# Three PSUM banks for each kind of score in the feature attention, and a new instruction order in the grouped-query attention of a decoder kernel

## The chip, the cores and the metric

The kernel runs on one core of one Trainium2 chip. The time is the device time of one execution in microseconds; the number reported is the median of the runs. A difference of less than 0.2% (about 6 us here) can't be told from no change.

## The reference

Two pre-norm layers over x of 64 x 64 x 256 values, each x = x + block(layernorm(x)). The change touches the first two of the six blocks.

```python
# block 1: grouped-query attention, 16 query heads, 4 key heads of 128, causal
q, k, v = split(x @ w_qkv.T)
q = layernorm(q) * g + b; k = layernorm(k) * g + b      # per head
q = q * cos + rotate_half(q) * sin                      # k the same
attn = softmax(causal(q @ k.T / sqrt(128))) @ v
x = x + attn @ w_o.T
# block 2: attention over features, 8 heads of 8 positions
qh, kh, vh = (a.reshape(b * 8, 64 // 8, 256) for a in (q, ctx, ctx))
sm = softmax(einsum('bdm,bdn->bmn', qh, kh) / sqrt(8))  # 256 x 256 scores
x = x + einsum('bmn,bcn->bcm', sm, vh).reshape(b, 64, 256)
```

## The kernel before

The 64 sequences are 32 tiles of 128 rows (two sequences). x stays in SBUF (`x_all`). Each block runs over the 32 tiles with one instruction stream per engine, written by hand, and counted semaphores between them. `over_tiles` (L35) unrolls two tiles (block 1) or four (block 2) per loop turn; in the source `t` is the tile and `step(t, ...)` the code of a tile on one engine. What stands in `step` on each engine is the order of the work; a wait is `wait_ge(semaphore, count)`, and `wait_used` (L48) is the wait for a buffer to be free.

**Block 1, `attention_gqa` (L545).** In step t, the scores and softmax of tile t run beside the projections of tile t+1 (the names `keys`, `value`, `queries`, `square_keys`, `keys_raw`, `rotate_query` with t+1), the output projection of tile t-1 (`at_.values`, `at_.project`) and the transposed layernorm rows of tile t+2. PSUM's eight banks are all in use; `QBANK` gives the banks 2, 1, 0, 3 to the four groups g of four query heads. On TensorE (PE) the step opens with `keys` (L103 to L105 with a_wk), `value`, the eight transposes of the probabilities of t-1 (L391), `query_sums` (L904, L905: sums of squares that give each query's variance), `bias_scores` (L896: the part of the scores that comes from the layernorm's bias, needed only at `s2m`), `key_sums` (L867), `scores` (L916), and then values, queries and projections. VectorE (DVE) runs `keys_raw` (L744, L745), the variance `vq` (L796), `keys_summed` (L750, L752), `s2m` (L800), the statistics of t+2, the scaled scores s (L809, L814), `low` (L437, the low half of an fp16 split), `take_max` (L357), then the query rotation: `rotate_query` (L764) and `add_swapped` (L769) for four groups, the denominator (L375), and `ln.low` (L280), which releases the next tile's `keys`. GpSimd (POOL) raises vq to the power -1/2 (L645, `rq`), does the same for the keys, then `swapped_part` (L627) and `squares_low` (L632) per group, `subtract_max` (L361) and `normalise` (L381). ScalarE (ACT) reads each query group out of PSUM: two squares (L684, L685) and two copies that swap halves (L688, qsw); between groups 1 and 2 stand the exponential (L370), the copy of v (L678) and the second `high` (L431, the high half of the split), and at the end `ln.high` (L276).

**Block 2, `attention_features` (L1159).** A tile has XU = 16 units (one head of one sequence). Softmax needs a maximum per column before the exponential, so each unit's scores are computed twice: raw scores of tile t+1 (L1458, then the maximum on DVE, L1394) and, with the maxima fed back through DRAM as a row of q, shifted scores of tile t (L1462, then the exponential on ACT, L1363), which PE issues in alternation in `both_scores`. At step u of tile t PE does the raw scores of the unit u+4 of tile t+1 and the shifted scores of the unit u+2 of tile t. `wait_scores` waits until the maximum has left the raw bank, `wait_shifted` until the exponential has left the shifted bank. Every second step adds `values` (L1495, the weighted sums, 0.62 us for eight matmuls), and the steps 11 and 13 one half each of `gather_output` (L1519). Banks 0 to 3 hold raw scores, 4 and 5 shifted ones, 6 the sums and 7 the gathered output and the negated maxima. ACT interleaves with its 16 exponentials: `shifts` (L1340, the negated maxima), `values_out` (L1346, twice, each behind a `values` of PE), and after the exponential of unit 14 `inverse_out` (L1351), which waits for PE's second gather, issued in step 13. The ring `e` of ES = 8 buffers lets the exponential of a unit u that is a multiple of four start only behind the `values` of the group two before it.

```python
s1_ps = lambda u: ps[:, u % 4, :].rearrange("p (c n) -> p c n", n=DM)
s2_ps = lambda u: ps[:, 4 + u % 2, :]
...
if not (isinstance(t, int) and XU * t + u < 4):
    pe.wait_ge(mx_ready, XU * t + u - 3)
...
if not (isinstance(t, int) and XU * t + u < 2):
    pe.wait_ge(e_ready, XU * t + u - 1)
```

## Time and profile before

| what | value |
|---|---|
| median of 3 runs | 3075.42 us (3070.69 to 3077.81) |
| the profiled execution | 3078.19 us, its span 3076.4 us |
| block 1, from its first to its last scores | about 72 to 892 us, 32 tiles, 26.4 us from tile to tile |
| block 2 | about 940 to 1406 us, 32 tiles, 13.37 us from tile to tile in most of it |
| TensorE clock granted, mean | 0.958 of full speed |

The profile is one execution as the hardware profiler saw it. A row of its timeline gives start, duration, engine, line and operation, and in brackets how long the engine had been idle and which instruction ended that. Busy shares are averages over stages with different limits, so each block is read by its own cycle: the time from an event of one tile to the same event of the next.

### The profile page before, as it was taken

How to read it: one execution, taken by the hardware profiler on the slowest of the kernel's cores; microseconds unless marked ns; L12 is line 12 of the kernel's file. 1: busy time of each engine (PE TensorE's matmuls, PEld its weight loads, DVE VectorE, ACT ScalarE, POOL GpSimd, SP SyncE). 2: the span in 40 equal slices, each digit the busy share in tenths (PEclk: the TensorE clock that was granted, in tenths of full speed). 3: DMA queues.
4: the chain of work that ended last, by engine and by line, in shares of the span. 5: the costliest groups of instructions: out<-in, count | busy, mean ns of one | idle time of the engine just before them, and what ended most of it. 6: DMA issues, size and time to landing. Idle time of an engine off the chain costs nothing. (4 is left out here: it accounts for less than half of the span.)

```text
span 3076.4 us, 86672 instructions
## 1 busy us (share of the span) xinstructions
PE 2646.2 (86%) x33275; PEld 1934.0 (63%) x33291; DVE 2017.7 (66%) x3674; ACT 1573.7 (51%) x2950; POOL 1405.2 (46%) x1522
## 2 busy tenths in 40 slices
PE   3888888888876888886779989999999999999576
PEld 2677777777751222222468867888888888888333
DVE  5888888888866788884878862343434343433697
ACT  3565555556544677772134433444444444444587
POOL 4888888888852223322434421222222222222487
PEclk9999999999996899997989989999999999999899
DMA  3000000000002232320011110000000000000000
GB/s 125 2 0 0 0 0 0 0 0 0 0 1 86 83 94 86 91 82 11 0 39 31 34 52 31 7 4 4 5 3 5 3 5 3 5 32 1 4 24 27
DMA packets 94668, 75.60 MB, mean 25 GB/s; under 512 B 17520, under 2 KB 88560, under 8 KB 93424
## 3 DMA queue, kind: packets, MB, share of 16 engines
q1 hardware_dynamic: 94576, 74.35, 7.9%
q8 instruction: 60, 0.98, 0.1%
q14 instruction: 32, 0.26, 0.0%
HBM read 55.97 MB, written 17.04 MB: 24 GB/s over the span
## 5 line engine op out<-in xcount | busy, mean ns | idle before, releaser
L1394 DVE TENSOR_REDUCE x_mx<-x_ps 128x2 f16<-128x512 f32 x512 | 332.8, 683 | 57.2 <-PE x_ps L1458 54.3
L1363 ACT ACTIVATE x_e<-x_ps 128x512 f32<-128x512 f32 x512 | 292.2, 596 | 55.1 <-PE x_ps L1462 38.1
L361 POOL TENSOR_TENSOR x1s<-x1s,x1mx 128x1024 f32<-128x1024 f32 x32 | 60.8, 1900 | 519.0 <-DVE x1mx L357 519.0
L1458 PE MATMUL x_ps<-x_k,x_q 32*128 32x256 f16 x1024 | 199.4, 292 | 80.9 <-ACT x_e L1363 48.0
L1722 ACT ACTIVATE x_q<-x_ps,x_q_bias,x_q_scale 128x128 f32<-128x128 f32 x512 | 185.7, 467 | 159.7 <-PE x_ps L105 159.7
L1458 PEld LDWEIGHTS x_ps<-x_k,x_q 32*128 32x128 f16 x1024 | 58.1, 93 | 269.4 <-DVE x_mx L1394 130.4
L431 ACT CAST x1oh<-x_ps 128x1024 f16<-128x1024 f32 x64 | 64.7, 1012 | 313.0 <-PE x_ps L423 313.0
L103 PE MATMUL a_ps<-ln_xha,a_wq 128*128 128x128 f16 x1024 | 180.3, 222 | 51.2 <-ACT a0v L678 44.0
L627 POOL TENSOR_TENSOR a_w<-a_qsw,a_tab 128x512 f32<-128x512 f32 x128 | 176.6, 1380 | 57.3 <-ACT a_qsw L688 56.0
L1462 PE MATMUL x_ps<-x_q,x_k 32*128 32x256 f16 x1024 | 201.0, 293 | 1.7 <-ACT x_e L1363 1.4
L280 DVE TENSOR_TENSOR ln_xlx<-x_ps,ln_xhx 128x256 f16<-128x256 f32 x32 | 13.6, 424 | 281.6 <-ACT x_xt L1714 281.6
L103 PE MATMUL x_ps<-x_chi,x_w 128*128 128x128 f16 x1024 | 181.4, 221 | 1.7 <-DVE x_z L1800 1.7
L769 DVE TENSOR_TENSOR a_u<-a_u,a_w 128x512 f32<-128x512 f32 x128 | 181.8, 1441 | 0.0
L104 PE MATMUL x_ps<-x_clo,x_w 128*128 128x128 f16 x1024 | 180.8, 221 | 0.0
L105 PE MATMUL x_ps<-x_chi,x_w 128*128 128x128 f16 x1024 | 180.7, 221 | 0.0
L105 PE MATMUL a_ps<-ln_xha,a_wq 128*128 128x128 f16 x1024 | 179.5, 221 | 0.0
L104 PE MATMUL a_ps<-ln_xla,a_wq 128*128 128x128 f16 x1024 | 179.4, 221 | 0.0
L105 PE MATMUL x_ps<-ln_xhx,x_w 128*128 128x128 f16 x1024 | 176.5, 220 | 0.0
L104 PE MATMUL x_ps<-ln_xlx,x_w 128*128 128x128 f16 x1024 | 176.5, 220 | 0.0
L103 PE MATMUL x_ps<-ln_xhx,x_w 128*128 128x128 f16 x1024 | 176.5, 220 | 0.0
L632 POOL TENSOR_TENSOR a_sql<-a_sq,a_sqh 128x512 bf16<-128x512 f32 x128 | 176.1, 1376 | 0.0
L1495 PE MATMUL x_ps<-x_e,x_vt 128*9 128x256 f32 x2048 | 175.8, 419 | 0.1
(369 smaller groups left out, 9144.1 us busy)
## 6 DMA issues: line engine op xcount, KB each, us to landing
x_q<-x_q_rows SPq DMA_DIRECT2D x32, 256.0 KB, 2.8
x_k<-x_k_rows SPq DMA_DIRECT2D x32, 256.0 KB, 3.1
a_stage<-in_x_w SPq DMA_DIRECT2D x32, 256.0 KB, 2.6
x_vt<-in_ctx_v SPq DMA_DIRECT2D x32, 144.0 KB, 2.3
stage<-in_x_wt SPq DMA_DIRECT2D x4, 1028.0 KB, 6.4
x_all<-in_x SPq DMA_DIRECT2D x8, 512.0 KB, 10.0
x_cf<-in_ctx SPq DMA_DIRECT2D x32, 128.0 KB, 2.1
x_q_rows<-x_xhl SPq DMA_DIRECT2D x32, 128.0 KB, 1.7
```

The costliest lines, as they stand in the source:

```text
L103: pe.matmul(out, a[0], b[0], start=start, stop=False)
L104: pe.matmul(out, a[0], b[1], start=False, stop=False)
L105: return pe.matmul(out, a[1], b[0], start=False, stop=stop)
L627: pool.tensor_tensor(by_head(w, g), by_head(qsw, g), table(QW), ALU.mult).then_inc(w_ready, 1)
L632: pool.tensor_tensor(by_head(sql, g), by_head(sq, g), by_head(sqh, g), ALU.subtract).then_inc(sql_ready, 1)
L769: dve.tensor_tensor(by_head(u, g), by_head(u, g), by_head(w, g), ALU.add).then_inc(uw_ready, 1)
L1363: act.activation(e[:, u % ES].rearrange("p c n -> p (c n)"), s2_ps(u), ACT.Exp, scale=XT ** -0.5).then_inc(e_ready, 1)
L1394: dve.reduce_max(mx[:, p % 2, c:c + 2], s1_ps(u), AX).then_inc(mx_ready, 1)
L1458: return pe.matmul(s1_ps(u)[:, c], q[r, p % 4, g, c * P:(c + 1) * P], k[r, p % 4, g], start=True, stop=True)
L1462: return pe.matmul(s2_ps(u)[:, c * DM:(c + 1) * DM], k[r, p % 4, g, c * P:(c + 1) * P], q[r, p % 4, g], start=True, stop=True)
L1495: last = pe.matmul(o_ps[32 * jj:32 * jj + VC, g % 2, :], vt[:, p % 2, n, u, :], e[:, u % ES, n, :], start=n == 0, stop=n == KC - 1)
L1722: last = act.activation(q[:, i, :], ps[:, bank(4 + g), h * P:(h + 1) * P], ACT.Identity, scale=q_scale[:, i:i + 1], bias=q_bias[:, i:i + 1])
```

## The change

Block 2: raw scores get three banks (0 to 2) and shifted scores three (3 to 5), by the table `turn`, which gives the unit u of every tile its bank; `gone[u]` is how many units back the same bank was used last. The shifted scores are issued for the unit u+3 in place of u+2. ACT copies the shifts of the next tile after unit 8 in place of 9, and DVE takes the reciprocals after unit 6 in place of 5. Since 16 isn't a multiple of three, `turn` ends in (0, 1, 2, 1): `gone` is 3 for the units 3 to 14, 2 for the units 15 and 1, and 4 for 0 and 2.

Block 1: `u_ready` becomes four semaphores, one for each query group, so that the groups may be rotated in another order. PE issues `bias_scores` at the head of the step, ahead of `keys`. ACT splits `square` in two: group 0 is swapped ahead of its squares, the second `high` stands ahead of the exponential. DVE takes `vq` ahead of `keys_raw`; joins the two halves of the keys (`keys_joined`) only ahead of `take_max`; and has a new order from there to the end of the step.

```diff
-        s1_ps = lambda u: ps[:, u % 4, :].rearrange("p (c n) -> p c n", n=DM)
-        s2_ps = lambda u: ps[:, 4 + u % 2, :]
+        turn = (0, 1, 2) * 4 + (0, 1, 2, 1)
+        gone = [next(n for n in range(1, XU) if turn[u - n] == turn[u]) for u in range(XU)]
+        s1_ps = lambda u: ps[:, turn[u], :].rearrange("p (c n) -> p c n", n=DM)
+        s2_ps = lambda u: ps[:, 3 + turn[u], :]
...
-                    if u == 9 and has_next:
+                    if u == 8 and has_next:
                         shifts(t + 1, 0)
...
-                    if u == 5 and started(t):
+                    if u == 6 and started(t):
                         reciprocals(t - 1)
...
-                if not (isinstance(t, int) and XU * t + u < 4):
-                    pe.wait_ge(mx_ready, XU * t + u - 3)
+                if not (isinstance(t, int) and XU * t + u < 3):
+                    pe.wait_ge(mx_ready, XU * t + u + 1 - gone[u])
...
-                if not (isinstance(t, int) and XU * t + u < 2):
-                    pe.wait_ge(e_ready, XU * t + u - 1)
+                if not (isinstance(t, int) and XU * t + u < 3):
+                    pe.wait_ge(e_ready, XU * t + u + 1 - gone[u])
...
-                for u in range(2):
+                for u in range(3):
                     only_shifted(0, 0, u)
...
-                    after, w = divmod(u + 2, XU)
+                    after, w = divmod(u + 3, XU)
```

Of block 1 the diff's waits (the orders follow below):

```diff
+        u_ready = [sem(f"u_ready{g}") for g in range(4)]
...
+            def swap_query(t, g):
+                act.wait_ge(q_ready, 4 * t + g + 1)
                 wait_used(act, w_ready, t, 1, 4, g + 1)
...
                 dve.wait_ge(qsw_ready, 4 * t + g + 1)
+                dve.wait_ge(sqh_ready, 4 * t + g + 1)
                 wait_used(dve, at_.sc_ready, t, 1)
-                dve.tensor_tensor(by_head(u, g), heads_of(ps[:, QBANK[g], :]), table(QC), ALU.mult).then_inc(u_ready, 1)
+                dve.tensor_tensor(by_head(u, g), heads_of(ps[:, QBANK[g], :]), table(QC), ALU.mult).then_inc(u_ready[g], 1)
...
             def step(t, p, has_next):
                 before = not (isinstance(t, int) and t == 0)
+                bias_scores(t, p)
                 if has_next:
                     keys(t + 1, 1 - p)
                     value(t + 1, 1 - p)
                 if before:
                     at_.transpose(pe, t - 1, at_.x_done)
                 query_sums(t)
-                bias_scores(t, p)
```

Block 1, PE, before, in the loop, from the last of the query sums to the scores (a_kt the keys, a_bq the bias table, a_u the rotated queries):

```order
L904 MATMUL a_ps<-onesb,a_sqh 128x1
L905 MATMUL a_ps<-onesb,a_sql 128x1
L53 ISA [waits a0_kt_ready]
L896 MATMUL a_ps<-a_kt,a_bq 128x512 [waits a0_ol_ready]
L867 MATMUL a_ps<-ones,a_sqk 128x1 [waits a0_sqk_ready]
L867 MATMUL a_ps<-ones,a_sqk 128x1 x3
L916 MATMUL a_ps<-a_kt,a_u 64x64 [waits a0_pt_ready,a0_uw_ready]
```

And with the change, on PE, across the border between two steps (a_wk the key weights):

```order
L270 MATMUL a_ps<-ident,ln_xna 128x128 [waits a0_xl_ready,a0_xn_ready,a0_u_ready2]
L270 MATMUL a_ps<-ident,ln_xna 128x128
L41 UNCONDITIONAL_BRANCH
L41 ISA
L53 ISA [waits a0_kt_ready]
L909 MATMUL a_ps<-a_kt,a_bq 128x512 [waits a0_ol_ready]
L861 REGISTER_ALU
L103 MATMUL a_ps<-ln_xha,a_wk 128x128 [waits a0_u_ready1,a0_xl_ready]
```

The bias scores left the place between query sums and key sums and stand ahead of the keys, which wait for `ln.low`.

Block 1, DVE, before, in one step from the maximum to the end (a_u rotated queries, a_w their swapped part, a0ol the low half, ln_xla the next rows):

```order
L357 TENSOR_REDUCE a0mx<-a0s 128x16
L764 TENSOR_TENSOR a_u<-a_ps,a_tab 128x4x2x64 [waits a0_sc_ready,a0_qsw_ready]
L757 TENSOR_TENSOR a_kt<-a_kt,a_ps 128x512 [waits a0_rkb_ready]
L758 TENSOR_TENSOR a_kt<-a_kt,a_tab 128x512 [waits a0_chain]
...
L375 TENSOR_REDUCE a0den<-a0e 128x16 [waits a0_e_ready]
L377 RECIPROCAL a0rden<-a0den 128x16 [waits a0_p_ready,a0_chain]
L437 TENSOR_TENSOR a0ol<-a_ps,a0oh 128x1024 [waits a0_oh_ready]
L262 TENSOR_SCALAR ln_xna<-x_all,ln_mva,ln_rstda 128x256 [waits a0_mv_ready,a0_rstd_ready]
...
L455 SCALAR_TENSOR_TENSOR x_all<-a_ps,x_all 128x256 [waits a0_y_ready]
L280 TENSOR_TENSOR ln_xla<-a_ps,ln_xha 128x256 [waits a0_xh_ready]
L769 TENSOR_TENSOR a_u<-a_u,a_w 128x4x2x64 [waits a0_w_ready,a0_u_ready] x2
```

And with the change, the same piece:

```order
L761 TENSOR_TENSOR a_kt<-a_kt,a_tmp 128x512 [waits a0_kraw_ready]
L357 TENSOR_REDUCE a0mx<-a0s 128x16 [waits a0_chain]
...
L262 TENSOR_SCALAR ln_xna<-x_all,ln_mva,ln_rstda 128x256 [waits a0_mv_ready,a0_rstd_ready]
L437 TENSOR_TENSOR a0ol<-a_ps,a0oh 128x1024 [waits a0_oh_ready]
L375 TENSOR_REDUCE a0den<-a0e 128x16 [waits a0_e_ready]
L377 RECIPROCAL a0rden<-a0den 128x16 [waits a0_p_ready,a0_chain]
...
L779 TENSOR_TENSOR a_u<-a_u,a_w 128x4x2x64 [waits a0_w_ready,a0_u_ready1]
L280 TENSOR_TENSOR ln_xla<-a_ps,ln_xha 128x256 [waits a0_xh_ready]
L774 TENSOR_TENSOR a_u<-a_ps,a_tab 128x4x2x64 [waits a0_sc_ready,a0_sqh_ready,a0_qsw_ready]
L455 SCALAR_TENSOR_TENSOR x_all<-a_ps,x_all 128x256 [waits a0_y_ready]
```

`keys_joined` (L761) moved down to just ahead of the maximum; the normalisation and the second `low` moved ahead of the denominator; the rotation of group 3 and the addition to x moved behind `ln.low` (L280). In block 2 the order of PE's instructions stays as it was in the loop; what changes there are banks and the counts in the waits, as the diff shows.

## Rows read from the trace of the kernel before

**Rows 1.** Windows view: blocks 1 and 2; busy PE, PEld, DVE, ACT, POOL, then clock.
```profile
77.00:924.00 847.00, 713.13 (x9538) 588.94 (x9535) 704.70 (x894) 480.63 (x774) 668.70 (x464) 0.98 0.00 0
...
924.00:1409.00 485.00, 403.09 (x4664) 111.12 (x4664) 374.48 (x707) 339.45 (x671) 133.56 (x224) 0.88 0.28 83
```

**Rows 2.** Timeline of PE, one tile of block 1: start, duration, idle before.
```profile
410.20 0.23 PE L103 MATMUL a_ps<-ln_xha,a_wk 128*128 128x128 f16 x1 [1.67 <-DVE ln_xla L280]
...
414.52 1.10 PE L896 MATMUL a_ps<-a_kt,a_bq 128*128 128x512 f32 x2
...
415.46 0.95 PE L867 MATMUL a_ps<-ones,a_sqk 128*128 128x1 f32 x8
...
425.74 1.13 PE L416 MATMUL a_ps<-a0pt,a0v 64*128 64x256 f32 x8
...
436.51 0.23 PE L103 MATMUL a_ps<-ln_xha,a_wk 128*128 128x128 f16 x1 [1.68 <-DVE ln_xla L280]
```

**Rows 3.** Timeline of DVE, the same tile of block 1.
```profile
414.78 0.17 DVE L796 TENSOR_SCALAR a_vq<-a_ps 128x16 f32<-128x16 f32 x1
...
418.47 1.23 DVE L809 TENSOR_TENSOR a0s<-a_ps,a_rq 128x1024 f32<-128x1024 f32 x1
...
422.39 1.21 DVE L357 TENSOR_REDUCE a0mx<-a0s 128x16 f32<-128x1024 f32 x1
...
429.15 1.22 DVE L375 TENSOR_REDUCE a0den<-a0e 128x16 f32<-128x1024 f32 x1 [0.57 <-ACT a0e L370]
...
435.02 0.69 DVE L764 TENSOR_TENSOR a_u<-a_ps,a_tab 128x512 f32<-128x512 f32 x1 [0.44 <-ACT a_qsw L688]
...
435.96 0.41 DVE L280 TENSOR_TENSOR ln_xla<-a_ps,ln_xha 128x256 f16<-128x256 f32 x1
```

**Rows 4.** Timeline of POOL, the same tile of block 1.
```profile
415.03 2.90 POOL L645 TENSOR_TENSOR a_rq<-a_vq,mhalf 128x16 f32<-128x16 f32 x1 [2.88 <-DVE a_vq L796]
...
425.67 2.35 POOL L361 TENSOR_TENSOR a0s<-a0s,a0mx 128x1024 f32<-128x1024 f32 x1
```

**Rows 5.** Timeline of ACT, the same tile of block 1.
```profile
428.06 1.06 ACT L370 ACTIVATE a0e<-a0s 128x1024 f32<-128x1024 f32 x1 [2.50 <-POOL a0s L361]
...
429.50 1.00 ACT L431 CAST a0oh<-a_ps 128x1024 f16<-128x1024 f32 x1
...
435.01 0.37 ACT L276 CAST ln_xha<-a_ps 128x256 f16<-128x256 f32 x1
```

**Rows 6.** Timeline of ACT, one tile of block 2: units 12 to 15 and 0.
```profile
1207.79 1.71 ACT L1363 ACTIVATE x_e<-x_ps 128x512 f32<-128x512 f32 x3
...
1210.34 0.37 ACT L1351 COPY x_inverse<-x_ps 128x256 f32<-128x256 f32 x1 [0.84 <-PE x_ps L1519]
...
1210.61 1.20 ACT L1363 ACTIVATE x_e<-x_ps 128x512 f32<-128x512 f32 x2
```

**Rows 7.** Timeline of PE, block 2: step 12, gather, values of step 14, step 0.
```profile
1208.44 0.28 PE L1458 MATMUL x_ps<-x_k,x_q 32*128 32x256 f16 x1 [0.30 <-ACT x_e L1363]
...
1209.64 0.64 PE L1519 MATMUL x_ps<-x_rec_rows,x_gather 128*32 128x256 f32 x8
...
1210.53 0.62 PE L1495 MATMUL x_ps<-x_e,x_vt 128*9 128x256 f32 x8
...
1211.96 0.26 PE L1458 MATMUL x_ps<-x_k,x_q 32*128 32x256 f16 x1
```

**Rows 8.** Timeline of DVE, block 2: the maxima that end with step 9.
```profile
1206.74 1.29 DVE L1394 TENSOR_REDUCE x_mx<-x_ps 128x2 f16<-128x512 f32 x2
```

**Rows 9.** The page: the exponentials of block 2 and their waits.
```profile
L1363 ACT ACTIVATE x_e<-x_ps 128x512 f32<-128x512 f32 x512 | 292.2, 596 | 55.1 <-PE x_ps L1462 38.1
```

**Rows 10.** Block 2: a window at half clock; the two inverses after that of rows 6.
```profile
1028.00:1042.00 14.00, 13.12 (x118) 2.54 (x110) 10.07 (x20) 8.83 (x18) 2.10 (x4) 0.51 0.31 90
...
1224.62 0.37 ACT L1351 COPY x_inverse<-x_ps 128x256 f32<-128x256 f32 x1 [0.84 <-PE x_ps L1519]
...
1238.00 0.37 ACT L1351 COPY x_inverse<-x_ps 128x256 f32<-128x256 f32 x1 [0.84 <-PE x_ps L1519]
```

More of the change, by code:

```diff
@@ L712, in step @@
                     value(t + 1, 1 - p)
-                if before:
-                    at_.high(act, t - 1, 1, not has_next)
-                if has_next:
-                    square(t + 1, 2)
-                    square(t + 1, 3)
+                    for g in (2, 3):
+                        square(t + 1, g)
+                        swap_query(t + 1, g)
                 if further(t):
@@ L833, in step @@
                     at_.add(dve, t - 1)
-                if further(t):
-                    ln.low(dve, t + 2, p)
                 if has_next:
```

44 lines of the change are left out of this document (27 added, 17 removed).

## The prediction

> **What bounds the kernel now.** The windows view of the two blocks comes first. In block 1 no engine is full: DVE is busy 705 of 847 us, PE 713, POOL 669 [rows 1]. So a cycle through several engines sets the pace, and the timeline of one tile is read for it. Its start K is the first key matmul, at 410.20; the next is at 436.51, so a tile takes 26.31 us [rows 2]. Going back from there: keys wait 1.68 us for DVE's `ln.low` at 435.96, and start 0.55 us behind its start [rows 2, 3]. `ln.low` follows ACT's `ln.high` at 435.01, the end of a queue that runs without a gap from the exponential at 428.06, 6.95 us [rows 5]. The exponential waits 2.50 us for POOL's subtraction, whose start at 425.67 lies 2.39 us ahead [rows 4, 5]. The maximum is at 422.39, the scaled scores at 418.47, and these stand behind POOL's power, which starts 0.25 us behind `vq` at 414.78 and takes 2.90 us [rows 3, 4].
>
> Block 2 moves in units. There PE must wait in step u for the exponential of unit u, and ACT waits for PE at three kinds of place; the longest is 0.84 us for the inverse, behind PE's second gather [rows 6]. Two inverses are 13.38 us apart (1224.62 to 1238.00 [rows 10]; most of the 31 distances are 13.37), and ACT, PE and that wait form the cycle. DVE ran its maxima with time to spare: those of step 9 end at 1208.03 [rows 8], which nothing at that moment waits for with four banks.
>
> **Block 1, part by part.** *Bias scores.* They leave the place ahead of the key sums, where they hold PE for 0.94 us (414.52 to 415.46), and go into the 1.68 us that PE idles ahead of the keys [rows 2]. The idle time hides them; without that cover they would cost 0.94 us. Key sums, scores, the values and all of PE's queue behind them come 0.94 us earlier.
> *vq first.* In the row it starts as soon as the query sums are out, so it gains at most 0.1 us. But the keys' two multiplications now run beside POOL's power. The power ends at 417.93 [rows 4]; the scores are out 0.94 us earlier than 418.4; so the scaled scores start about 7.75 us behind K in place of 8.27 [rows 3]: 0.5 us gained.
> *ACT.* The second `high`, 0.9 us, leaves the queue behind the exponential. It waits for the second values, which end at 426.87 now [rows 2] and 0.94 earlier then, so it ends 16.7 us behind K and the exponential starts there, in place of 17.86 [rows 5]. `ln.high` then could stand at K + 22.7. Group 0's swap ahead of its squares frees POOL sooner, so that its subtraction waits for the maximum alone. That ends at 12.19 + 1.21 - 0.5 + 0.7 = K + 13.6 (the 0.7 is the join, below), and 2.39 us later, at K + 16.0, the exponential could start: the second `high` comes last.
> *DVE.* From the scaled scores to `ln.low` it takes 17.49 us (418.47 to 435.96). Out of that go the rotation of group 3 (0.61 of its 0.69 us) and the addition to x (0.33), both moved behind `ln.low`, and the gaps of 0.57 and 0.44 us [rows 3], since the exponential and the swaps are 1.2 to 2 us earlier. Joining the keys comes in, 0.7 us with its own wait. That makes 17.49 - 0.61 - 0.33 - 0.57 - 0.44 + 0.70 = 16.24 us, so `ln.low` at K + 23.99 and the next keys at K + 24.54. DVE is then the end of the chain, ahead of ACT's K + 22.7 by 1.3. A tile costs 26.31 - 24.54 = 1.77 us less. DVE is left with almost no slack and every late hand-over counts in full, so I take 1.6. The ends: 0.5 (only the earlier scores remain) and 2.1 (the waits in front of `vq` shrink too). Over 31 tile distances: **-49.6 us**, between -16 and -65.
> The further waits (squares ahead of a rotation, four semaphores in place of one) are for things long done at that place: nothing.
>
> **Block 2, part by part.** *The shifted scores a unit further ahead.* Before, step u waits for the exponential of unit u. With three banks in strict turn, unit u+3 would wait for the same one, so ACT gets slack and PE loses nothing. But the turn isn't strict at the tile's end: `gone` is 2 for the units 15 and 1. Unit 15 is issued in step 12 and waits for the exponential of unit 13; unit 1 of the next tile is issued in step 14 and waits for that of unit 15. And ahead of the exponential of unit 15 in ACT's queue stands `inverse_out`, which waits for the gather of step 13. So a chain that ran side by side becomes serial. In times behind the exponential of unit 12 (1207.79):
> - Unit 13 starts at 0.56 (three in 1.71 us); step 12 follows a start by 0.65 us [rows 6, 7], so it comes at 1.21 in place of 0.65, and the second gather ends at 3.05 in place of 2.49 (1210.28).
> - The inverse starts 0.06 behind it, at 3.11. Unit 15 starts 0.27 us later, at 3.38 (1210.34 and 1210.61). Step 14 takes another 0.75: 4.13. Before it was at 2.42, 0.32 us ahead of its values [rows 7].
> - Its values end 0.94 us later, at 5.07; the ring lets unit 0 start at 5.13; step 0 of the next tile comes at 5.83. Before, 1211.96, which is 4.17 [rows 7].
> So a tile costs 1.66 us more. The inverse's own length is unchanged: what is lost is PE's idle time while ACT does it. In stretches at half clock PE is the longer partner; there only the wait from the gather's end to step 14 is added, 0.06 + 0.27 + 0.75 = 1.07 us. Of the 31 distances some 24 lie at full clock and 7 at half, as in the window of [rows 10]: 24 x 1.66 + 7 x 1.07 = **+47.3 us**. Bounds: +10, if the first part is all (0.3 a tile, where step 12 hides), and +60.
> *The raw scores with three banks.* Step 11 (unit 15 again) now waits for the maximum of step 9, which ends at 1208.03 [rows 8]. A step with a gather takes PE 0.9 us, so step 11 can start at 1208.44 - 0.9 = 1207.5 at most: it is up to 0.5 us late, but step 12 is late by 0.56 anyway and the reciprocals' move brings these maxima forward by up to 0.6. I take nothing, at most 0.2 a tile.
> *Reciprocals and shifts one unit later or earlier*: the sums' DMA has 0.6 us more time to land, on DVE, which isn't the bound: nothing. No DMA is moved past another on SP's queue.
> *The clock.* It was at half speed in parts of block 2 (0.88 on average [rows 1]); one such dip makes a tile 14.28 in place of 13.37 us (1210.34 to 1224.62 [rows 6, 10]). The fall came behind stretches in which PE had idled among short groups. With 1.07 us more idle time a tile I count nine more dips of 0.91: **+8.2 us**, between 0 and +75.
>
> **The sum.** -49.6 + 47.3 + 8.2 = +5.9 us. Against the profiled execution's 3078.2 us that is 3084; its time is 2.8 above the median, so I give the median's: 3075.4 + 5.9 = **3081 us**. Two large terms cancel.
>
> A rule speaks for more than this. The exponentials of block 2 wait 38.1 us for shifted scores [rows 9]. The Trainium skill, "Perfetto Trace Analysis", Optimization Strategy, says that the same gap repeated on an engine that should be saturated can mean too little PSUM for the next tile, and by that rule a third bank should return those 38.1 us. In the tile that I followed these waits of 0.29 us stand ahead of waits for the values, so they are already inside something longer; the trace doesn't bear the rule out here.
>
> **Rivals.**
> - *The third bank pays* (0.13). ACT's 38.1 us [rows 9] go and the serial chain hides in the slack so won: 3075.4 - 49.6 - 38.1 = 2988; if the two only cancel, 3026. For it: 38.1 us is real idle time. Against it: PE's gap behind the gather is ordered by counts, and slack can't remove it.
> - *The new order in block 1 brings little* (0.15). Place: DVE's queue between maximum and `ln.low`. If a rotation waits for its swap there, or the join sits fully on the path, 0.3 us a tile remain: -9 + 55.5 gives 3122, slower. It decides from 1.3 us of new waits on DVE a tile.
> - *The clock falls for good in block 2* (0.12), slower. A window at half clock has 118 PE instructions in 14 us, where a tile has 4664 / 32 = 146 [rows 1, 10]: 17.3 us a tile, so 24 tiles lose some 4.5 us each with part of the wait, in place of 1.66: -49.6 + 108 + 7.5 gives 3141, half of it 3110. It decides where the mean clock of the block falls below 0.75. The Trainium skill, "TensorE: Matmul & The Clock Gate", section on psum-queue depth-cycling, describes just this: small idle times of PE while banks are cycled make the clock swing between its two levels. The dips of rows 10 agree; that it would stay down no row shows.
> - *The forecast* (0.60): both as worked out, 3055 to 3105.
>
> **How the numbers follow.** About 6 us, 0.2%, is what can be told from no change. The forecast's own share is a third each side of that: 0.20 faster, 0.20 the same, 0.20 slower. The first rival adds 0.13 to faster, the other two 0.27 to slower: 0.33, 0.20, 0.47. The range runs from the first rival's 3026 to the second's 3122; 2988 and the clock's 3141 stay out: 3025 to 3125.
>
> **What would show it.** Block 1: keys 24.5 to 25 us apart, the bias scores inside PE's old gap, the exponential 16.7 us behind the keys, DVE without idle time from scaled scores to `ln.low`. Block 2: inverses about 15 us apart, a PE wait of about 1 us for ACT in step 14, and no more exponentials that wait for L1462's successor. Wrong would be: inverses 13.4 us or less apart (the chain doesn't bite), or keys still 26 us apart. The mean clock of block 2 decides the third rival.

## The result, and the profile after

The changed kernel takes **3271.3 us** (median of 4 executions, 3271.11 to 3271.54) against 3074.8 for the kernel before on the same chip: ratio 1.064, 95% interval 1.0622 to 1.0659. Slower by 6.4%, where 3081 us and a range of 3025 to 3125 stood. The page of the kernel after, its span and the clock row of its 40 slices:

```profile
span 3269.4 us, 86732 instructions
...
PEclk9999999999955555555698998999999999999799
```

Eight slices in a row are at half clock. The windows view (columns as in [rows 1]) puts them on block 2; block 1 now ends 19 us earlier, so the windows are 77 to 905 and 905 to 1600:

```profile
77.00:905.00 828.00, 724.91 (x9530) 587.66 (x9530) 745.33 (x897) 479.60 (x771) 683.80 (x463) 0.98 0.00 0
905.00:1600.00 695.00, 607.33 (x4664) 139.05 (x4664) 389.97 (x706) 322.17 (x671) 134.12 (x223) 0.50 0.20 58
```

In block 2 the clock is 0.50, so 1.2 GHz, up to its last tile, against 0.88 in [rows 1]. Counting by the inverse, copied once a tile: the first comes at 966.8 (982.4 before), the last at 1602.8 (1413.6), and 1666.6 us follow (1662.8). So of the 193.0 us that the two spans differ, block 1 gives back 15.6, the 31 tile distances of block 2 cost 204.7, and 3.8 lie behind.

**Block 1.** One tile of the kernel after, PE's timeline, which answers to [rows 2]:

```profile
401.77 0.23 PE L103 MATMUL a_ps<-ln_xha,a_wk 128*128 128x128 f16 x1
...
426.07 0.41 PE L270 MATMUL a_ps<-ident,ln_xna 128*128 128x128 f32 x2 [1.49 <-DVE a_u L774]
426.66 1.12 PE L909 MATMUL a_ps<-a_kt,a_bq 128*128 128x512 f32 x2 [0.18 <-issue]
427.62 0.22 PE L103 MATMUL a_ps<-ln_xha,a_wk 128*128 128x128 f16 x1
```

and DVE's, ACT's and POOL's of the same tile, for [rows 3], [rows 5] and [rows 4]:

```profile
409.52 1.23 DVE L819 TENSOR_TENSOR a0s<-a_ps,a_rq 128x1024 f32<-128x1024 f32 x1 [0.65 <-PE a_ps L929]
410.78 1.83 DVE L824 TENSOR_TENSOR a0s<-a0s,a_s2m 128x1024 f32<-128x1024 f32 x1
...
413.89 1.19 DVE L761 TENSOR_TENSOR a_kt<-a_kt,a_tmp 128x512 f32<-128x512 f32 x1
415.11 1.22 DVE L357 TENSOR_REDUCE a0mx<-a0s 128x16 f32<-128x1024 f32 x1
...
426.92 0.42 DVE L280 TENSOR_TENSOR ln_xla<-a_ps,ln_xha 128x256 f16<-128x256 f32 x1
```

```profile
418.84 1.06 ACT L370 ACTIVATE a0e<-a0s 128x1024 f32<-128x1024 f32 x1
...
426.51 0.37 ACT L276 CAST ln_xha<-a_ps 128x256 f16<-128x256 f32 x1 [1.46 <-PE a_ps L270]
```

```profile
406.53 2.90 POOL L646 TENSOR_TENSOR a_rq<-a_vq,mhalf 128x16 f32<-128x16 f32 x1 [1.44 <-DVE a_vq L805]
```

The tile takes 25.85 us (401.77 to 427.62). The scaled scores start 7.75 us behind K (409.52 - 401.77) as worked out, and DVE runs without a gap from there to `ln.low`. But it needs 17.40 us for that stretch, not 16.24. The bias scores nearly fit into PE's gap, not wholly: the transposes of the layernorm rows (L270) now wait 1.49 us for DVE's rotation of group 2, the bias scores start behind them at 426.66, and the keys follow 0.70 us behind the start of `ln.low` in place of 0.55. The same transposes release ACT's `ln.high`, which ends at 426.88, K + 25.1, only 0.04 us ahead of `ln.low`; so the two ways to `ln.low`, over DVE's queue and over ACT, arrive together, where DVE's was to be 1.3 us the longer.

**Block 2.** ACT's timeline, two inverses and the exponential behind the second, for [rows 6] and [rows 10]:

```profile
1260.80 0.37 ACT L1366 COPY x_inverse<-x_ps 128x256 f32<-128x256 f32 x1 [2.85 <-PE x_ps L1534]
...
1281.66 0.37 ACT L1366 COPY x_inverse<-x_ps 128x256 f32<-128x256 f32 x1 [2.76 <-PE x_ps L1534]
1281.92 0.60 ACT L1378 ACTIVATE x_e<-x_ps 128x512 f32<-128x512 f32 x1
```

and PE's around it, second gather, step 14 and its values, for [rows 7]:

```profile
1280.51 1.08 PE L1534 MATMUL x_ps<-x_rec_rows,x_gather 128*32 128x256 f32 x8
...
1282.67 0.37 PE L1473 MATMUL x_ps<-x_k,x_q 32*128 32x256 f16 x1 [1.08 <-ACT x_e L1378]
...
1283.21 1.04 PE L1510 MATMUL x_ps<-x_e,x_vt 128*9 128x256 f32 x8
```

The wait of 1.08 us in step 14 is the serial chain, where it was worked out as 1.07 (its three parts, 0.06, 0.27 and 0.75, make 1.08). But a tile takes 20.9 us (1260.80 to 1281.66), where 15 stood at full clock.

### The profile page after: what moved, and what is told of

The parts are those of the page before. It is cut to its first block and busy times, and to the rows that moved or that the text cites. A ratio compares the mean times of both kernels' runs of the same rounds, so it can differ in the third digit from the quotient of the medians.

```text
span 3269.4 us, 86732 instructions
## 1 busy us (share of the span) xinstructions
PE 2866.3 (88%) x33291; PEld 1962.1 (60%) x33291; DVE 2074.2 (63%) x3674; ACT 1557.5 (48%) x2950; POOL 1423.2 (44%) x1522
## 5 line engine op out<-in xcount | busy, mean ns | idle before, releaser
L1409 DVE TENSOR_REDUCE x_mx<-x_ps 128x2 f16<-128x512 f32 x512 | 345.8, 689 | 247.8 <-PE x_ps L1473 246.5
L1378 ACT ACTIVATE x_e<-x_ps 128x512 f32<-128x512 f32 x512 | 272.6, 594 | 131.2 <-PE x_ps L1510 128.5
L1473 PE MATMUL x_ps<-x_k,x_q 32*128 32x256 f16 x1024 | 248.6, 399 | 89.1 <-ACT x_e L1378 44.9
L1477 PE MATMUL x_ps<-x_q,x_k 32*128 32x256 f16 x1024 | 288.8, 405 | 2.4 <-ACT x_e L1378 2.1
L361 POOL TENSOR_TENSOR x1s<-x1s,x1mx 128x1024 f32<-128x1024 f32 x32 | 60.9, 1902 | 519.1 <-DVE x1mx L357 519.1
L1510 PE MATMUL x_ps<-x_e,x_vt 128*9 128x256 f32 x2048 | 265.9, 612 | 0.2 <-ACT x_e L1378 0.2
L628 POOL TENSOR_TENSOR a_w<-a_qsw,a_tab 128x512 f32<-128x512 f32 x128 | 190.5, 1488 | 6.6 <-ACT a_qsw L692 6.6
L779 DVE TENSOR_TENSOR a_u<-a_u,a_w 128x512 f32<-128x512 f32 x128 | 191.8, 1519 | 2.3 <-POOL a_w L628 1.2
L280 DVE TENSOR_TENSOR ln_xlx<-x_ps,ln_xhx 128x256 f16<-128x256 f32 x32 | 13.6, 424 | 281.6 <-ACT x_xt L1729 281.6
L633 POOL TENSOR_TENSOR a_sql<-a_sq,a_sqh 128x512 bf16<-128x512 f32 x128 | 191.4, 1495 | 0.0
L250 POOL TENSOR_TENSOR ln_vex<-ln_mvx,ln_epsx 128x1 f32<-128x1 f32 x64 | 12.3, 192 | 394.6 <-DVE ln_mvx L257 394.6
L103 PE MATMUL x_ps<-ln_xhx,x_w 128*128 128x128 f16 x1024 | 176.5, 220 | 0.0
```

The source lines that it names most:

```text
L103: pe.matmul(out, a[0], b[0], start=start, stop=False)
L628: pool.tensor_tensor(by_head(w, g), by_head(qsw, g), table(QW), ALU.mult).then_inc(w_ready, 1)
L633: pool.tensor_tensor(by_head(sql, g), by_head(sq, g), by_head(sqh, g), ALU.subtract).then_inc(sql_ready, 1)
L779: dve.tensor_tensor(by_head(u, g), by_head(u, g), by_head(w, g), ALU.add).then_inc(uw_ready, 1)
L1378: act.activation(e[:, u % ES].rearrange("p c n -> p (c n)"), s2_ps(u), ACT.Exp, scale=XT ** -0.5).then_inc(e_ready, 1)
L1409: dve.reduce_max(mx[:, p % 2, c:c + 2], s1_ps(u), AX).then_inc(mx_ready, 1)
```

## The experiments

Two things were open: what holds the clock down, and where block 1's gain went. A row that the forecast had not looked at gave a theory for the first. In the kernel (`rows(u)`) the operands of a unit lie on the 32 partitions that begin at 32 x (unit mod 4), so its matmuls use these 32 rows of TensorE, called its row group here. Before, step u issues raw scores u+4 and shifted scores u+2: row groups u and u+2 (mod 4); the next step uses u+1 and u+3, so the four groups of two steps are disjoint. With shifted scores u+3 a step uses u and u+3, the next u+1 and u, and both use group u. In steps without values between them the next step's products follow at once. PE in the kernel after, half clock, steps 5 and 6 of a tile (raw products only; the shifted ones stand between):

```profile
1291.30 0.39 PE L1473 MATMUL x_ps<-x_k,x_q 32*128 32x256 f16 x1
...
1291.32 0.59 PE L1473 MATMUL x_ps<-x_k,x_q 32*128 32x256 f16 x2
...
1291.50 0.42 PE L1473 MATMUL x_ps<-x_k,x_q 32*128 32x256 f16 x1
...
1292.26 1.04 PE L1510 MATMUL x_ps<-x_e,x_vt 128*9 128x256 f32 x8
```

The values start 0.96 us behind the first product. In the kernel e6 below, which has three and three banks as well but shifted scores of u+2, also at half clock:

```profile
1177.04 0.39 PE L1473 MATMUL x_ps<-x_k,x_q 32*128 32x256 f16 x1
...
1177.06 0.39 PE L1473 MATMUL x_ps<-x_k,x_q 32*128 32x256 f16 x1
...
1177.23 0.42 PE L1473 MATMUL x_ps<-x_k,x_q 32*128 32x256 f16 x1
...
1177.24 0.42 PE L1473 MATMUL x_ps<-x_k,x_q 32*128 32x256 f16 x1
...
1177.59 1.04 PE L1510 MATMUL x_ps<-x_e,x_vt 128*9 128x256 f32 x8
```

Here both steps run side by side and the values start 0.55 us behind. In e7 below, where the shifted scores are those of u+3 again but the raw ones those of u+5, so that the groups are disjoint, it is 0.55 us too (1259.53 to 1260.08, half clock). The Trainium skill, "TensorE: Matmul & The Clock Gate", part on packing small matmuls (The mechanism), says that a weight load overlaps with running matmuls only where its row group differs. By that rule the two steps of the kernel after can't fully overlap, and the 0.96 against 0.55 us agree.

All kernels, in one table. "Last inverse" and "rest" (the span behind it) are from the profiled execution, "clock" is the mean of block 2 there (905 us to about the last inverse). "Pad" marks the kernels whose rest is longer; it is explained at e18. The kernels ran on several chips, each beside the kernel before, whose median was 3068 to 3081 us; so times from different chips are best compared by their ratios.

| kernel | median us | ratio to before (95%) | last inverse | clock | rest |
|---|---|---|---|---|---|
| before | 3074.8 | | 1413.6 | 0.88 | 1663 |
| the change | 3271.3 | 1.0640 (1.0622, 1.0659) | 1602.8 | 0.50 | 1667 |
| e1 block 1 only | 3060.2 | 0.9943 (0.9920, 0.9966) | 1389.3 | 0.88 | 1671 |
| e2 block 2 only | 3291.6 | 1.0720 (1.0685, 1.0755) | 1626.0 | 0.50 | 1663 |
| e3 inverse late | 3233.6 | 1.0505 (1.0475, 1.0534) | 1567.3 | 0.50 | 1667 |
| e4 waits alone | 3192.7 | 1.0380 (1.0348, 1.0412) | 1522.5 | 0.61 | 1667 |
| e5 filler | 3287.1 | 1.0686 (1.0656, 1.0716) | 1616.1 | 0.50 | 1669 |
| e6 shifted u+2 | 3120.5 | 1.0156 (1.0129, 1.0182) | 1391.6 | 0.82 | 1722 pad |
| e7 raw u+5, inverse late | 3185.5 | 1.0369 (1.0342, 1.0396) | 1457.1 | 0.72 | 1722 pad |
| e8 raw u+3 | 3101.5 | 1.0085 (1.0062, 1.0107) | 1443.3 | 0.75 | 1668 |
| e9 raw u+5 | 3242.0 | 1.0533 (1.0504, 1.0562) | 1521.4 | 0.64 | 1722 pad |
| e10 u+2, reciprocals later | 3057.1 | 0.9944 (0.9925, 0.9963) | 1336.8 | 0.93 | 1724 pad |
| e11 e1, inverse late | 3036.8 | 0.9883 (0.9861, 0.9906) | 1372.7 | 0.91 | 1663 |
| e12 e1, reciprocals later | 3051.2 | 0.9932 (0.9910, 0.9954) | 1380.5 | 0.91 | 1663 |
| e13 wait in step 12 | 3069.9 | 0.9993 (0.9979, 1.0008) | 1406.1 | 0.87 | 1662 |
| e14 change, both later | 3097 or 3235 | see there | 1567.9 | 0.50 | 1667 |
| e15 raw u+5, both later | 3150.4 | 1.0225 (1.0194, 1.0255) | 1430.6 | 0.80 | 1726 pad |
| e16 e1, both later | 3034.0 | 0.9858 (0.9835, 0.9882) | 1365.8 | 0.94 | 1666 |
| e17 u+2, both later | 3047.7 | 0.9886 (0.9854, 0.9918) | 1328.3 | 0.93 | 1722 pad |
| **e18** e17, one instruction more | **2988.6** | 0.9737 (0.9712, 0.9763) | 1322.2 | 0.94 | 1665 |

### The two blocks apart: e1, e2

```diff
 e1: block 1 as changed, all of block 2's lines as before
 e2: block 1 as before, block 2 as changed
```

> The change to block 1 alone; block 2 as before. Theory A (the whole loss lies in block 2, block 1 gained about 19 us, as its keys are 25.7 us apart in place of 26.4): about 3056 us, ratio 0.994, block 2 in about 13.4 us a tile at a mean clock near 0.88. Rival (block 2 fell to half clock because of something that block 1's new order leaves behind): still above 3200 us.

> Edit: block 1 as before the change, block 2 as changed. If the two parts are independent, the loss of block 2 stands alone: 3271 us plus the 15 us that block 1 gained, so 3286 us (3280 to 3295), with inverses 21.0 us apart at half clock. If the state of the clock in block 2 came from how block 1 now ends, near 3075 to 3150 us.

e1 gives 3060.2 us, 0.6% under before, as theory A had it; e2 gives 3291.6, with inverses 21.0 us apart. Against the kernel before on their own chips that is -17 and +223, +206 together, where the change has +197: the parts are nearly independent, and the loss is block 2's alone. In e1 too the first tile of block 2 runs mostly at half clock (0.56), and the clock is back by the second; in the changed kernel it doesn't come back.

### The waits: e3, e4, e5, e13

```diff
 e3, in the change (ACT):
-                    if u == 14 and not first:
+                    if u == 15 and not first:
                         inverse_out(t - 1)
 e4, in e1 (PE, wait_shifted, two shifted banks):
-                    pe.wait_ge(e_ready, XU * t + u - 1)
+                    pe.wait_ge(e_ready, XU * t + u - 1 + (u in (0, 14)))
 e13: as e4, with (u == 14)
 e5, in the change (PE, both_scores):
+                if u2 == 1:
+                    for _ in range(8):
+                        scores(p1, u1, 0)
                 wait_shifted(t2, p2, u2)
```

> The whole change, with the copy of the inverse moved from behind the exponential of unit 14 to behind that of unit 15, so that PE's step 14 no longer waits for gather, inverse and exponential in a row. Theory A (that serial wait, 1.08 us of PE idling a tile at half clock, is what keeps the clock down): the clock returns to 0.85 or more in block 2, tiles of 13.4 to 14 us, 3055 to 3080 us. Rival B (three raw banks are too few, or the unit 15 and 1 waits as such): half clock stays, tiles of 19 to 20 us, 3210 to 3250 us.

> Block 1 changed, block 2 with its old four and two banks and its old unit order; only the two waits of the change are put in: step 12 waits for the exponential of unit 13, step 14 for that of unit 15. Theory A (the two waits alone do it): tiles of about 21 us at half clock, 3240 to 3290 us. Rival B (the bank split or the raw side does it): tiles of about 15 us at full clock from the serial chain alone, about 3105 us.

> The whole change, with eight more raw-score matmuls (L1473's form, the same result written again) in step 14 ahead of the wait for the exponential, so that PE is active in the gap. They need about 0.9 us at full clock. Theory A1 (the idle time brings the clock down): block 2 runs mostly at full clock and its tiles take the serial chain's 15 us, 3090 to 3130 us. Rival A2 (the clock is down for another reason, as the low share of the array that these small matmuls use): half clock stays, and the fillers cost 0 to 1.2 us a tile: 3270 to 3310 us.

> Edit: the new block 1 with the old block 2, and one wait only: the shifted scores of unit 14, in step 12, wait for the exponential of unit 13 in place of unit 12. The wait in step 14, which closes the serial chain with the products and the inverse, is left out. With both waits: 3192.7 us. Theory A (the serial chain in step 14 is what costs): 3060 to 3085 us. Theory B (any wait of about 0.4 to 1 us that stops TensorE for the newest exponential brings the clock down, the products have nothing to do with it): 3120 us and more.

e4 has the old banks and the old row groups, and only the two waits of the change. ACT's inverses in it, one distance at full clock and one at half:

```profile
1163.62 0.37 ACT L1364 COPY x_inverse<-x_ps 128x256 f32<-128x256 f32 x1 [0.84 <-PE x_ps L1532]
1178.47 0.37 ACT L1364 COPY x_inverse<-x_ps 128x256 f32<-128x256 f32 x1 [0.84 <-PE x_ps L1532]
1197.57 0.37 ACT L1364 COPY x_inverse<-x_ps 128x256 f32<-128x256 f32 x1 [1.93 <-PE x_ps L1532]
1217.30 0.37 ACT L1364 COPY x_inverse<-x_ps 128x256 f32<-128x256 f32 x1 [1.92 <-PE x_ps L1532]
```

14.85 us (14.6 to 15.1 in all tiles at full clock) is the serial chain as the prediction worked it out: 13.37 + 1.66 = 15.03. 19.7 us is a tile at half clock. Of 132 us over e1 the chain itself can explain 31 x 1.66 = 51; the rest is clock, 0.61 in place of 0.88. Neither forecast for e4 came true: 3192.7 us lies between them. e13 shows which wait does it: the one in step 12 alone costs 10 us (15 by the ratios), so nearly all comes with the one in step 14, where the inverse and the exponential behind it lie in the cycle. (The one in step 14 without the other was not run.) Taking only the copy out of that cycle (e3) gives 38 us, but the block stays at half clock with 19.9 us a tile: the wait is not all of it. e5 fills the time of the wait with matmuls that write the same scores again. TensorE's waits for exponentials fall from 40.5 to 11.0 us (1000 to 1560 us, waits view), and the clock stays at half, 21.5 us a tile: TensorE's idle time at that place alone isn't what holds it, as rival A2 had it. Its longer code also brought 178 instruction fetches in place of 60, but not in block 2: from 900 to 1620 us both kernels have 16.

### The row groups: e6, e7, e8, e9

```diff
 e6, in the change (PE):       after, w = divmod(u + 2, XU)      in place of u + 3
 e7, in e3 (PE, DVE):          ahead, v = divmod(u + 5, XU)      in place of u + 4
 e8, in e1 (PE, DVE):          ahead, v = divmod(u + 3, XU)      in place of u + 4
 e9: e7 with the inverse at u == 14
 (left out here: the units issued ahead of the loop, XL for the raw and range(...) for the shifted scores, follow these distances)
```

> Edit: the whole change with its three and three banks, but a step takes the shifted scores of unit u+2 again, not of u+3. In a step the raw scores use row group u mod 4 and the shifted ones (u+2) mod 4, the next step the two others, as before the change; unit 1's wait for its late shifts falls in step 15, behind the products that the reciprocals need. Theory A (row groups: with u+3 two neighbouring steps share a group, so their matmuls no longer run beside each other, the stage takes longer at half clock and the clock stays down): the inverses come 13.4 to 13.6 us apart, the granted clock of block 2 is mostly above 0.9, about 3060 us (3050 to 3080). Theory B (three raw banks, so that each raw matmul waits for the maximum of two steps before, hold the stage back): inverses stay 18.5 us apart or more at half clock, above 3190 us.

> Edit: the whole change with its three and three banks and the shifted scores of u+3, but the raw scores and maxima of unit u+5 in place of u+4, and the inverse copied in step 15 so that ACT's wait is out of the way. A step uses row groups (u+1) mod 4 and (u+3) mod 4, the next the two others. Theory A (row groups): the steps overlap again, the clock comes back, tiles of 13.4 to 14 us, 3050 to 3090 us. Theory B (the depth of the shifted scores, or the three banks of each kind, not the row groups): half clock as with the late inverse alone, tiles of 18.5 to 20 us, 3190 to 3240 us.

> Edit: block 1 as changed; block 2 as in the kernel before, with four raw banks and two shifted ones and the shifted scores of u+2, but the raw scores of unit u+3 in place of u+4. A step then uses row groups (u+3) mod 4 and (u+2) mod 4, and shares one of them with the next step; no bank, no inverse and no depth of the shifted scores is changed. Theory A (row groups): the collision alone is enough, half clock through most of block 2, tiles of 18.5 to 20 us, 3190 to 3250 us. Theory B (banks or depth of the change): nothing like it here, 13.4 us tiles, about 3060 us.

> Edit: the whole change, but the raw scores and maxima of unit u+5; the inverse stays in step 14, so the serial chain of reciprocal products, inverse and exponentials is whole while the row groups of neighbouring steps are disjoint. Theory A (row groups hold the clock down, the chain only costs its own 1 to 1.7 us per tile): tiles of 14.6 to 15.1 us where the clock is full, a mix with half-clock tiles as with the waits alone, 3100 to 3200 us. Theory B (the chain holds the clock down by itself): 20 to 21 us tiles at half clock all through, 3240 to 3275 us.

e8 has no bank and no wait of the change, only a shared row group. It falls into stretches of either kind, here tiles of 19.4 to 19.6 us, then tiles of 13.4 (windows view):

```profile
1204.00:1280.00 76.00, 72.33 (x583) 16.70 (x583) 48.13 (x89) 42.40 (x84) 17.07 (x29) 0.53 0.22 65
1280.00:1350.00 70.00, 59.70 (x767) 17.93 (x763) 60.30 (x115) 55.33 (x111) 21.36 (x36) 1.00 0.31 91
```

So a shared group costs nothing at full clock (13.4 us a tile, as in e1) and lengthens a tile at half clock. e1's first tile, the nearest to a clean one at half clock, takes 17.1 us at a clock of 0.56; tiles at 0.50 that differ in the raw lookahead, and with it the row groups, compare better: 19.9 us in e3 and 18.7 in e7, 21.0 in the change and 19.95 in e9. That is 1.0 to 1.2 us a tile, about what three pairs of steps at 0.41 us (0.96 - 0.55) make. And once e8 has fallen to half clock it stays there for three or four tiles on end, where e1's falls after the first tiles last 3.5 to 14 us; then it comes back. Alone the shared group costs 41 us against e1, more than theory B had and far less than theory A's 3190, so both forecasts missed: the collision needs something more to hold the clock down.

e7 against e3 and e9 against the change differ in the raw lookahead alone, which makes the groups disjoint (and takes a step from the time in which a raw bank must come free). The last inverse comes 110 and 81 us earlier, and the clock rises from 0.50 to 0.72 and 0.64. Both run times are 54 us longer than they should be, for the reason found at e18; less that, 3131 and 3188 us. e7 is then between its two theories, e9 within its theory A and within 5 us of e4: with disjoint groups the change costs what the two waits alone cost.

e6 gave neither theory's number. Without the 54 us it is at 3066, which is theory A's time, but not its tiles (14.2 us on average, not 13.4 to 13.6) nor its clock (0.82, not above 0.9). Its block 2 has a wait that in e1 is much smaller (waits view, 965 to 1390 us: us in all, times, longest; e6, then e1):

```profile
PE x_ps L1473 <- DVE x_mx L1409: 37.2, 45, 2.0
...
DVE x_rec L1414 <- DMA x_den<-x_o: 32.8, 20, 5.2
```

```profile
DVE x_rec L1412 <- DMA x_den<-x_o: 26.8, 24, 5.7
...
PE x_ps L1471 <- DVE x_mx L1407: 5.5, 9, 1.4
```

In both, DVE stands in front of the reciprocals until the denominators have landed, and the maxima stand behind. With four raw banks PE hardly notices; with three it waits 37.2 us for them.

### Inverse and reciprocals later: e10, e11, e12, e14, e15, e16, e17

```diff
 DVE, with three raw banks (e10, e14, e15, e17):
-                    if u == 6 and started(t):
+                    if u == 8 and started(t):
                         reciprocals(t - 1)
 DVE, with four (e12, e16): u == 5 becomes u == 7
 ACT (e11, e14 to e17): inverse_out at u == 15
 e10 = e6 + reciprocals; e17 = e10 + inverse; e14 = e3 + reciprocals; e15 = e7 + reciprocals
 e11, e12, e16 = e1 + inverse, + reciprocals, + both
```

> Edit: the whole change with the shifted scores of u+2 (as e6), and the reciprocals in the maxima's step 8 in place of step 6. With u+2 alone the kernel took 3120 us, and VectorE stood 32.8 us in all waiting for the denominators' transfer ahead of the reciprocals, in long waits of up to 5 us, and TensorE 37.2 us for maxima queued behind them. Theory A (three raw banks leave no room for that one wait): moved two steps back, the wait of TensorE for maxima falls to under 12 us in all and the time to 3060 to 3085 us. Theory B (the bank order itself, units 15 and 1 only two behind their predecessors, is what stops TensorE): no change, 3110 to 3130 us.

> Edit: the new block 1 with the old block 2, and in that the inverse copied in step 15 in place of 14. ACT waited 33.1 us in all for the reciprocal products ahead of the inverse (0.84 us a tile), and the exponentials behind it. If that wait is on the chain of PE and ACT, tiles of 13.4 us shrink by 0.2 to 0.5 us and the time is 3045 to 3055 us; if the chain only makes the wait up elsewhere, 3060 us as without the edit.

> Edit: the new block 1 with the old block 2, and in that the reciprocals in step 7 in place of 5. VectorE waited 26.8 us in all for the denominators, TensorE 5.5 us for maxima. With four raw banks the first should hardly reach TensorE: 3055 to 3060 us; if the dips of the clock (seven or eight in this stage) come from these waits, up to 20 us less, 3040 us.

> Edit: the whole change, with the inverse copied in step 15 and the reciprocals in the maxima's step 8. Left of block 2's faults is then the row group that neighbouring steps share, and the waits in steps 12 and 14 without the copy behind them. Theory A (the shared row group is enough to keep the clock from coming back): half clock through most of block 2, tiles of 19.5 to 20 us, 3200 to 3240 us. Theory B (the long waits for denominators and products were what kept it down): a mix or full clock, 3050 to 3120 us.

> Edit: as the kernel with both later, and the raw scores and maxima of unit u+5, so that neighbouring steps use disjoint row groups, with the shifted scores of u+3 kept. Theory A (row groups): full clock over most of the stage, 3040 to 3090 us, at least 100 us under the kernel that shares a group. Theory B (row groups don't matter once the waits are gone): within 20 us of that kernel, either way. A raw lookahead of five with three banks also leaves a raw matmul one step less between the maximum that frees its bank and itself, which may cost what the groups give: then 3100 to 3190 us, with waits of TensorE for maxima above 20 us in all.

> Edit: new block 1, old block 2, with the inverse in step 15 and the reciprocals in step 7. The inverse alone gave 3036.8 us, the reciprocals alone 3051.2 us, neither 3060.2 us. If the two add up: 3028 us (3020 to 3035). If both only remove the same dips of the clock: 3037 us as with the inverse alone.

> Edit: the whole change with the shifted scores of u+2, inverse in step 15, reciprocals in step 8; three and three banks, row groups disjoint. Theory A (row groups and the waits are all there is, the banks cost nothing): 3025 to 3045 us, as the best version with the old banks. Theory B (three raw banks cost something by themselves): 3050 us and more.

e10 is 63 us under e6 although PE still waits 20.9 us for maxima, more than theory A allowed; the inverses are 12.0 to 12.2 us apart in most of the block, less than the kernel before ever had. So three and three banks *can* pay. In the old block 2 the late inverse gives 23 us (e11), the late reciprocals 9 (e12), both 26 (e16); by the ratios 18, 3 and 26, of which the 3 can't be told from nothing. The late inverse takes the full-clock tile from 13.4 to 13.2 us, and with both no dip of the clock is left between 1000 and 1340 us.

e14 is the whole change with both moves; what is left in it is the shared row group and the waits of the units 15 and 1, without the copy behind them. Its eight executions fall into two groups: 3096.4 to 3119.9 us (four) and 3232.4 to 3237.3 us (four), with nothing between, on one chip and with the same data; the interval that goes with the first group is a ratio of 1.0043 to 1.0116. The profiled one is of the second: half clock from end to end, 19.9 us a tile, as in e3 (3229 to 3236 us). In a tile of its PE timeline no wait is longer than 0.76 us. No trace was kept of the first group; its clock over the whole program is 0.93 to 0.94, against 0.875 to 0.877. e15, the same with disjoint groups, has nothing of this in its four executions (3144 to 3158). Without its 54 us it is at 3096, the first group's time, so theory A's 100 us hold only against the second group. So with a shared group and the waits of the units 15 and 1 the block can run in two ways, and where it keeps to half clock it does so to the end; the changed kernel, with its long wait in step 14, did so in each of its four executions. The shared group isn't enough for that: e8 starts at half clock too and is back at full after three tiles. What in e14 decides between the two, and whether the waits or the three banks must join the shared group, no run shows.

e17 brings the last inverse to 1328 us, 37 us before e16, and still takes 14 us longer, so neither of its theories fits. That contradiction led to the last run.

### One instruction: e18

The waits view of e17 has, for 1750 to 2750 us, in a stage that no edit touches, TensorE standing still for nothing that the profile shows; its queue of instruction fetches counts 177, where e1's and the change's count 60:

```profile
PEld x_ps L391 <- issue: 52.0, 13, 4.4
```

```profile
q8 instruction: 177, 2.90, 0.4%
```

All six kernels marked "pad" have this, and in all six TensorE's program is one instruction shorter ahead of that stage's loop (9568 instructions of the built program stand ahead of it, against 9569 to 9574 in the unmarked ones; e5 has 150 more). The count of fetches alone is not the price: e5 has 178, and what follows its last inverse takes 1669 us, no more than in others; its stops at L391 add up to 7.4 us, not 52.0.

```diff
 e18, in e17 (PE, head of block 2):
                 pe.wait_ge(zeroed, 3)
+                pe.wait_ge(zeroed, 3)
```

> Edit: the kernel with shifted u+2 and both the inverse and the reciprocals later (e17, 3047.7 us), and one redundant wait more at the head of block 2's TensorE program, on a semaphore that is already there. Theory A (one instruction fewer ahead of the last attention stage moved its loop so that TensorE fetches instructions in every turn): the instruction fetches fall from 177 to 60, what follows the last inverse from 1722 to about 1666 us, and the time to 2992 us (2985 to 3000). Theory B (that stage is slow for another reason, such as the clock or what block 2 leaves behind): 3047 us again.

The fetches of e18:

```profile
q8 instruction: 60, 0.98, 0.1%
```

and ACT's inverses in it, 11.8 and 12.1 us apart:

```profile
1257.61 0.37 ACT L1366 COPY x_inverse<-x_ps 128x256 f32<-128x256 f32 x1
1269.38 0.37 ACT L1366 COPY x_inverse<-x_ps 128x256 f32<-128x256 f32 x1
1281.46 0.37 ACT L1366 COPY x_inverse<-x_ps 128x256 f32<-128x256 f32 x1
```

2988.6 us: theory A to 4 us. One redundant wait is worth 59 us between the two medians, which come from two chips, 46 us by the ratios; in the traces what follows the last inverse goes from 1722 to 1665 us. This is also the best version found, 2.6% under the kernel before. Against e16, the best with the old banks, its last inverse comes 44 us earlier and its ratio is 0.974 in place of 0.986: that is what three and three banks give once the rest is out of the way. It keeps all of block 1, the three and three banks and their order; it undoes the deeper lookahead and moves the inverse and the reciprocals.

The Trainium skill, "Runtime: NRT & Kernel Launch", section Instruction fetch mechanics, gives TensorE room for 2048 instructions, refilled in blocks of 256. An estimate from that page: the loop in question, 1491 instructions, spans 6 or 7 such blocks by where it begins, of 8. The 60 fetches agree that loops normally stay inside: by the same estimate TensorE's 12,696 instructions make 50 such blocks, each fetched about once. Why one instruction tips it over no run here shows.

## Why the prediction was wrong, step by step

- **The clock term, +8.2 us (bounds 0 to +75), was the step that failed.** Block 2 cost 205 us over its 31 distances. 47.3 were forecast for the chain; the other 157 come with the clock, 0.50 in place of 0.88, where 8.2 stood. The step counted dips of 0.91 us and took it that the clock comes back after each. Two things in the change keep it from coming back: the serial wait in step 14 (e4: 0.61) and the shared row group (0.50 in e3 and the change, 0.72 and 0.64 in e7 and e9). Neither holds it down to the end alone (e4, e8); why the chip grants half clock in such a stage is open, but TensorE's idle time in step 14 isn't the whole of it (e5).
- **The row groups were overlooked.** "ACT gets slack and PE loses nothing" weighed the deeper lookahead by waits alone. PE lost the overlap of neighbouring steps, at half clock 0.41 us a pair, three pairs a tile.
- **The price of a half-clock tile was too low.** Rival 3 took 17.3 us from a count of instructions in the window of [rows 10]. The nearest to a clean tile takes 17.1 (e1, clock 0.56); but one with the two waits takes 19.7 (e4), with the shared group 19.6 (e8), with both and the new banks 20.9. It is the rival of the clock that falls for good that came true, at 0.12, and its 108 us for the tiles should have been 205: the 31 distances were 20.5 us on average, against 13.9.
- **The serial chain was right.** Wait in step 14 worked out as 1.07 us, measured 1.08; full-clock tile 15.03, measured 14.6 to 15.1 (e4). At half clock the copy in step 14 costs 1.1 us a tile, as worked out (21.0 in the change, 19.9 in e3). The change never ran at full clock, so it never showed its 1.66.
- **Block 1's -49.6 us was mis-sized: -19.** DVE's queue is the chain, as forecast, though not 1.3 us longer than the way over ACT. The scaled scores came at K + 7.75 as worked out. The DVE stretch was worked out 1.16 us too short, and the bias scores, put wholly inside PE's gap, stick out by 0.15 us: 25.85 us a tile in place of 24.54. Groups view of 77 to 905 us; before, the two operations that joined the key rotation and added the shifted mask:

```profile
L758 DVE TENSOR_TENSOR a_kt<-a_kt,a_tab 128x512 f32<-128x512 f32 x31 | 45.9, 1482 | 1.1
L814 DVE TENSOR_TENSOR a0s<-a0s,a_s2m 128x1024 f32<-128x1024 f32 x32 | 45.3, 1417 | 1.1
```

 and after, the same two and the join:

```profile
L767 DVE TENSOR_TENSOR a_kt<-a_kt,a_tab 128x512 f32<-128x512 f32 x31 | 58.4, 1884 | 1.1
L824 DVE TENSOR_TENSOR a0s<-a0s,a_s2m 128x1024 f32<-128x1024 f32 x31 | 56.0, 1808 | 1.1
L761 DVE TENSOR_TENSOR a_kt<-a_kt,a_tmp 128x512 f32<-128x512 f32 x31 | 36.1, 1166 | 0.0
```

 The first two take 0.40 and 0.39 us more, the join 1.17 in place of the 0.7 assumed: 1.26 us a tile. So a part of the rival "the new order in block 1 brings little" came true: the join sits on the path and costs more than assumed. They are operations that read two tiles from SBUF, and in the new order they stand beside work of POOL, whose own products with tables went from 1.38 to 1.50 us. Those that read a tile from PSUM kept their length (the rotation of a query 0.68 in both). Other operations became shorter by their new neighbours: the normalisation (L262) went from 1.15 to 0.77 us, POOL's subtraction (L361) from 2.34 to 1.92. The Trainium skill, "GPSIMD Engine Reference", Specifications, says that POOL's SBUF interfaces are shared with DVE's and that they contend with DVE instructions that have two SBUF inputs or use both ports; the three groups above agree. No run moved one of them alone, so that this is the cause is argued, not shown.
- **Three raw banks, "nothing, at most 0.2 a tile": wrong by itself, hidden in the total.** It holds for maxima that are on time. It doesn't with the wait for the denominators in front of them: 37.2 us of PE's time, and the reciprocals' move by two more units brings some 60 us of run time (e6 against e10). Their move by one unit, costed at nothing, was in the right direction and too short. In the change itself, at half clock, PE waits 19.5 us in all for maxima.
- **The third-bank rule.** Rival 1 put its gain at 38.1 us and 2988 us. e18 reaches 2988.6, in another way, and that the numbers meet is luck: its full-clock tile is 1.5 us shorter than the 13.37 of before. In the kernels here the third bank pays when the lookahead stays at two, nothing serial is added and the reciprocals come later. The rule was weighed against by an argument from one gap, where a sum over the cycle was needed.

## What to carry to other kernels

A deeper lookahead is also a choice of which row group runs beside which: write down the groups of two neighbouring steps before changing a distance. Where a buffer count doesn't divide the loop, look for the places where the distance to the last user is shorter, and keep them away from steps that wait for a round trip (gather, DMA, reciprocal). When a stage already runs at half clock in parts (0.88 on average here), price an added wait also with half clock for the whole stage, and not only as a sum of dips: the tiles here took 20.9 us in place of 13.4.

## What was not expected of the hardware

- The same program on the same chip took about 3097 or 3235 us, by execution (e14); where it was profiled, at 3237, block 2 ran at half clock from end to end. Such a kernel's median says little.
- Moving the raw products by one unit, and with them their row group, took block 2's mean clock from 0.50 to 0.72 (e3, e7) with the same matmuls.
- One TensorE instruction fewer ahead of a loop brought 117 more instruction fetches and some 55 us, in a stage 400 us away from the edit; in e5 118 more brought about 2. Without e18 six experiments would have been read wrongly.
- Two of DVE's operations with two SBUF inputs took 1.42 us in the old order of block 1 and 1.81 in the new, 1.48 and 1.88.
